# Self attention on one Trainium2 core: the order of SyncE's transfers in a head, and the four copies of queries and keys by one repeated transfer each

## The reference

```
q = x @ Wq + bq ; k = x @ Wk + bk ; v = x @ Wv + bv        # x normalized before
q, k, v reshaped to (64, 1024, 32)                          # 4 batches x 16 heads
attn = softmax(einsum('bqd,bkd->bqk', q, k) * 8)
ctx  = einsum('bqk,bkd->bqd', attn, v)
```

## Time and profile before

| what | us |
|---|---|
| median of 3 runs (14980.4 to 15003.98) | 14988.53 |
| the profiled execution's own time | 14944.12 |
| its span, first to last instruction | 14942.4 |
| self attention: first score product of head 1 to that of head 63 | 1375.16 to 3509.80 |
| mean granted clock of TensorE over the span | 0.835 |

### The profile page before, as it was taken

How to read it: one execution, slowest core, us unless ns; L and a number is a source line. 1 busy time by engine, 2 the same in 40 slices (tenths; PEclk the granted TensorE clock), 3 DMA queues, 4 the chain that set the end, 5 groups by cost and what they waited for, 6 DMA issues and landing times. The chain is left out here.

```text
span 14942.4 us, 176465 instructions
## 1 busy us (share of the span) xinstructions
PE 12056.5 (81%) x56950; PEld 8114.4 (54%) x56950; DVE 7374.0 (49%) x13140; ACT 4440.9 (30%) x7890; POOL 6514.9 (44%) x5384
## 2 busy tenths in 40 slices
PE   8787888887668888888888888888888888888745
PEld 3553222223446666666666666666666666666622
DVE  0112333332236666666666666666666666666533
ACT  0111222221123333333333333333333333333310
POOL 0000000000036666666666666666666666666500
PEclk9888777777778888888888888888888888888766
DMA  3112222222123333333333333333333333333223
GB/s 75 52 44 52 54 54 52 51 54 60 64 68 78 79 80 83 83 80 80 80 78 82 83 81 79 80 80 80 83 83 80 80 81 80 80 83 83 62 72 102
DMA packets 1062473, 1096.94 MB, mean 73 GB/s; under 512 B 746498, under 2 KB 853762, under 8 KB 996882
## 3 DMA queue, kind: packets, MB, share of 16 engines
q1 hardware_dynamic: 988690, 1087.84, 30.3%
q10 hardware_dynamic: 73728, 8.42, 0.4%
HBM read 884.93 MB, written 210.76 MB: 73 GB/s over the span
## 5 line engine op out<-in xcount | busy, mean ns | idle before, releaser
L921 PE MATMUL c_pickps<-c_table,c_hot 128*128 128x112 f32 x16384 | 3468.2, 388 | 564.6 <-DVE c_over L1212 541.7
L921 PEld LDWEIGHTS c_pickps<-c_table,c_hot 128*128 128x128 f32 x16384 | 3299.6, 266 | 669.5 <-DVE c_over L1212 568.2
L1302 POOL TENSOR_TENSOR c_total<-c_total,c_over 128x384 f32<-128x384 f32 (+3 forms) x3584 | 3289.3, 918 | 465.3 <-DVE c_over L1212 185.7
L1302 POOL TENSOR_TENSOR c_total<-c_total,c_middle 128x1024 f32<-128x1024 f32 x512 | 1210.0, 2363 | 2854.6 <-DVE c_middle L1203 2854.6
L1189 DVE COPY_PREDICATED c_pickps<-c_upper,c_pickps 128x256 f32<-128x256 uint32 (+1 forms) x1024 | 799.0, 826 | 3352.2 <-PE c_pickps L921 3352.2
L1269 POOL IOTA c_digitrow<- 1x128 f32 x1 | 0.3, 255 | 4210.8 <-POOLq L65 4210.8
L1054 ACT ACTIVATE c_over<-c_place,c_thresholds 128x384 f32<-128x384 f32 (+3 forms) x3584 | 1589.3, 525 | 0.0
L1212 DVE TENSOR_TENSOR c_over<-c_over,c_pickps 128x384 f32<-128x384 f32 (+3 forms) x3584 | 1407.1, 452 | 0.0
L1037 ACT ACTIVATE c_place<-c_gateps 128x512 f32<-128x512 f32 x1024 | 611.4, 597 | 2674.4 <-PE c_gateps L894 2674.3
L894 PE MATMUL c_gateps<-c_qa,c_ka 128*128 128x512 f32 x2048 | 1105.2, 622 | 65.8 <-ACT c_place L1037 65.1
L960 PEld LDWEIGHTS c_softps<-c_v,c_probs 128*128 128x128 f32 x8192 | 1062.3, 208 | 138.2 <-issue 104.7
(11 more groups left out here) (213 smaller groups left out, 13740.9 us busy)
## 6 DMA issues: line engine op xcount, KB each, us to landing
c_hot<-t_digits SPq DMA_DIRECT2D x512, 1024.0 KB
t_tables<-c_tablesb SPq DMA_DIRECT2D x256, 256.0 KB, 5.6
c_table<-t_tables SPq DMA_DIRECT2D x1024, 56.0 KB, 2.3
a_q<-t_qa SPq DMA_DIRECT2D x384, 128.0 KB, 2.7
a_k<-t_ka SPq DMA_DIRECT2D x384, 128.0 KB, 3.1
c_kb<-t_kb SPq DMA_DIRECT2D x256, 128.0 KB, 6.2
t_digits<-c_anchorrows SPq DMA_DIRECT2D x128, 256.0 KB, 2.4
c_ka<-t_kb SPq DMA_DIRECT2D x128, 128.0 KB, 5.5
```

What stands on the lines that cost most here:

```text
L921: mm = nc.tensor.matmul(pick_ps[:, h // 4, 0:WIDTH, r * 8:(r + 1) * 8], hot[t % 2][:, h, :], table[s][:, :, :, t * 16 + h].rearrange("p l ...
L1302: nc.gpsimd.tensor_tensor(a, a, b, ALU.add).then_inc(s_add, 1)
```

## The change

Two edits in SyncE's program and one in what TensorE waits for. In a step, `send` of the previous head moves behind `load4` and `row`, and now stands in front of `load` only. And `load4` fills `q4[s]` and `k4[s]` by one transfer each in place of four: the source is the head's 32 x 1024 block repeated four times by an outer dimension of 4 that does not advance, the destination all 128 partitions. The bytes written are the same (512 KB per tile); the completion count that `peaks` waits for is 32 per head in place of 128.

```diff
                 for dst, src in ((q4[s], q_heads), (k4[s], k_heads)):
-                    for g in range(4):
-                        sp.dma_start(dst[32 * g:32 * g + DH, :], src[bass.ds(i, 1)].rearrange("a d t -> (a d) t")).then_inc(s_qk4[s], 16)
+                    rows = src[bass.ds(i, 1)].rearrange("a d t -> (a d) t").unsqueeze(0).to_broadcast([4, DH, SEQ])
+                    sp.dma_start(dst[:, :], rows).then_inc(s_qk4[s], 16)
...
             def step(i, s):
-                if not first(i):
-                    send(i - 1, 1 - s)
                 if not final(i, 2):
                     load4(i + 2, s)
                 if not final(i):
                     row(i + 1, 1 - s)
+                if not first(i):
+                    send(i - 1, 1 - s)
                 if not final(i, 2):
                     load(i + 2, s)
...
             def peaks(i, s, j):
                 if j == 0:
-                    pe.wait_ge(s_qk4[s], 128 * (i // 2 + 1))
+                    pe.wait_ge(s_qk4[s], 32 * (i // 2 + 1))
```

## The result

The changed kernel takes 14365.65 us (median of 4 runs, 14324.54 to 14397.55) against 14984.47 us for the kernel before (4 runs); the ratio is 0.9585, 95% interval 0.9553 to 0.9617. The forecast was 14370. The profiled execution took 14339.96 us against 14944.12.

A forecast was written before the change was run, and what follows sets the result against it. It took the self attention to be TensorE's, with a hole per head from the late row and a lower clock; 629 us less and 11 more gave -618, from 14988.5 to 14370 us, forecast range 14340 to 14420.

The forecast's parts named there:

- The head without the wait: Self attention: a head takes 24.28 us in place of 34.43, 10.15 less over 62 heads, 629 us.
- Hole and clock: TensorE between heads: of 10.15 us per head, 5.26 is idle time, about half hangs on the clock staying at 1.00.
- Rival A: Self attention: the hole goes but the clock falls all the same; 315 us less, 14674 us; chance 0.06.
- The order: SyncE's queue: with the row ahead of the send, the wait for the row goes whole, margin 4.5 us.
- The repeated transfers: SyncE's copies: eight issues become two, 3.5 us against 1.2; worth nothing by itself after the new order.
- The cap on the engines: DMA of the copies: an outer dimension of 4 confines them to 4 of 16 engines.
- The rate: DMA of the copies: 65.5 GB/s on 4 engines, 16.3 us taken for 1 MB per head.
- The margin: Row behind the copies on their engines: lands at about +21.5 us of a head, 2.8 us before needed.
- rival C: Self attention: copies at two engines' rate, 32.8 GB/s, 32 us, make the row late; 15310 us, slower; chance 0.07.
- The start: Self attention's start: the first peaks wait for the slower first copies, 11 us more, once.

The follow-up runs named there:

- six needless products: Kernel before, transfers unchanged, with six useless TensorE products at the head of each head's scores to fill the wait for the row: 14691.91 us, ratio 0.9812.
- order only: Kernel before with the new SyncE order alone, the copies staying eight transfers per head: 14361.54 us, ratio 0.9602.
- send ahead of the row: Changed kernel with the send put between the copies and the row: 14374.77 us, ratio 0.9607.
- two engines: Changed kernel with each tile of copies filled by two transfers of outer dimension 2 in place of one of 4: 14767.37 us, ratio 0.9876.
- needless products: Kernel before, transfers unchanged, with four useless TensorE products at the head of each head's scores, during the wait for the row: 14862.23 us, ratio 0.9932.

## Why the prediction was right

**The head without the wait** was the term that carried the sum, 24.28 us read from head 1 of the kernel before. Measured: 24.33 on the mean. Head 1 takes 24.28 again; a head takes 24.37 when the product behind it waits 0.21 us for ScalarE, which from head 2 on is at every other seam. 62 x (34.43 - 24.33) = 626 us against the 629 forecast.

**Hole and clock.** The prediction gave 5.26 us of a head's 10.15, read from one head, to the hole and the rest to the clock. The mean hole is 5.58 us (340.4 / 61). The six needless products separate the two over heads 1 to 62: 287 us of clock and 339 us of hole, with 4.9 x 62 = 303 and 5.26 x 62 = 326 expected. Each share was off by 13 to 16 us, and in opposite directions. Rival A is refuted: the clock stays up in the changed kernel, and it stays up with the row as late as before once the hole is filled.

**The order.** Right as a whole (order only: the full gain). Its text blamed send and copies together; the run with the send ahead of the row shows that the send was the lesser part of it: 0.55 us per head of stage, with the clock unharmed. The greater part was the copies, still to be issued when SyncE had done with waiting at `a_o`.

**The repeated transfers.** The cap on the engines was right: a share of 0.25 for 4 and 0.13 for 2. But only the order makes the time: with eight plain copies it is the same (14361.54 us). The rate was the mis-sized term: I took 65.5 GB/s and 16.3 us from `c_hot`'s 16.4 GB/s per engine; measured are 86 to 98 GB/s, about 21 to 25 per engine, and the copies are through some 13 us after their first issue, where 18 were expected. They end just before the row's issue (share 0.11 and below from then on), so the row never queued behind them, and lands sooner than it did before: median 1.7 us from issue, in place of 2.9. The margin was larger than forecast. What the prediction says of the row, that it stands behind the copies on their engines, is real: it costs nothing in this order, and 522 us in the old one. The same mis-sized rate stands in rival C, which for two engines had 32 us of copies and a kernel slower than before; measured, such copies make 14767 us.

**The start.** First copies to first score product: 27.6 us before (1319.18 to 1346.75), 37.3 after (1320.16 to 1357.46). That is 9.7 us for the 11 forecast. One thing was not in it: SyncE itself was held within one issue. That cost nothing here, as from the first peaks to the first score product it is 20.9 us in both kernels.

```profile
1324.10 10.05 SPq L408 DMA_DIRECT2D a_q<-t_qa  x1
```

The stage thus gives 619 us, as forecast (618). The profiled executions differ by 604. The missing 15 lie behind the stage: SyncE's first transfer of the next stage (L599) comes 618 us earlier, its first of the experts (L1503) 603, and the change touches nothing between them.

That the forecast of the median, 14370, lies 4 us from the measured 14366 is luck in part. The profiled execution took 14 us more than its forecast of 14326, and the median lay 26 us above that execution, not 44; the two errors nearly cancel.

## What to carry to other kernels

A queue that waits in order turns one late step into lateness for all behind it: for every wait of the issuing engine, ask what behind it has its data already, and put the transfer with the shortest path to the bounding engine where its data are fresh and nothing large is ahead of it, on the queue and on the DMA engines. Price a hole in TensorE's work above its length, for it is paid again in the clock, and a shorter hole saves little of that second part: per head the clock cost 4.7 us behind holes of 5.6 us (287 / 61), 4.5 behind 3.06 (272 / 61), and by an estimate 3.1 behind 1.69 (527 us more stage than the changed kernel has, less 63 x 3.70 of needless products and 103 of holes). In all that is 1.8, 2.5 and 2.8 times the hole; behind 0.69 us it was nothing. When a transfer is merged by a repeat, look at its outermost dimension; fewer issues can mean a fraction of the engines, and then only distance from the next urgent transfer makes it free.

## What the runs showed of the hardware that was not expected

- Holes well short of 5 us are enough for the clock: the mean is 0.89 with 1.69 us per head left over (behind needless products), 0.82 with 3.06 us, 0.79 with 5.6. With 0.69 us per head it stayed 1.00. Of single holes, the shortest with a fall behind it lasted 1.16 us, and so did the longest without one.
- Fewer DMA engines were each faster: 98 GB/s on four and about 49 on two, some 24.5 each, against 15.75 for the plain copies on sixteen (252 GB/s) and 16.4 for the `c_hot` load on eight. The `c_hot` load has its repeat inside and 8 KB rows; which of these makes it slow stays open.
- SyncE was held 10.05 us in the issue of one transfer when seven others with 1.6 MB had been issued before it within 4 us, two of them confined to four engines. The median of that line's issues is 0.62 us. With two engines a pair of issues in mid-stage took 3.83 us (2206.17). What exactly an issue waits for no run here shows.
